# The last two tiles of a fused projection kernel: broad passes of both first, then the narrow ones, and the last store issued by another engine

## The chip, the cores and the metric

The kernel runs on one core of a Trainium2 chip. A core has five engines that run their own instruction streams and meet through semaphores: TensorE (PE in the profile; its weight loads are listed apart as PEld), VectorE (DVE), ScalarE (ACT), GpSimd (POOL) and SyncE (SP), which here only issues transfers. The metric is the device time of one execution in microseconds, as a median over several runs.

## The reference, cut to what matters

The input x has 128 rows of the batch, 32 steps and 512 features, all in float32. For each element there is a base projection, a low-rank correction (LoRA) of two experts out of eight, chosen per token from logits with a bias for the row's own expert, a second projection by a matrix of signs, and the residual.

```python
base = jnp.einsum('btd,od->bto', x, W)
logits = jnp.einsum('btd,ed->bte', x, Wr) + bias[:, None, :]
topw, topi = jax.lax.top_k(logits, TOP_K)
weights = jax.nn.softmax(topw, axis=-1)
gates = jnp.sum(jax.nn.one_hot(topi, E) * weights[..., None], axis=-2)
h = jnp.einsum('btd,erd->bter', x, A)
lora_out = jnp.einsum('bter,bte,eor->bto', h, gates, B)
y = base + SCALING * lora_out
x = x + jnp.einsum('bsi,io->bso', y, sign) * jax.nn.softplus(scale)
```

## The kernel before, in words

**Tiles.** A tile is one step t of x: 128 batch rows by 512 features. There are 32 tiles (`TILES`), numbered 0 to 31. In its first 21 us the kernel multiplies W by the signs into one 512 by 512 matrix that also holds the residual, and B by the signs into b2. What is left for a tile is one product with a matrix `wide` of 648 columns, 8 for the logits, 128 for h (8 experts of rank 16) and 512 for the output, and one LoRA sum, the gated h times b2, added on top.

**Passes.** Each float32 product is made as three products of high and low parts (hi·hi, hi·lo, lo·hi), for each of four chunks of 128 features: 12 passes. The result of a tile lies in two PSUM banks: bank 0 holds logits, h and the first 256 output columns (8 + 128 + 256 = 392 columns), bank 1 the other 256 (`BANKS`). In the usual step each of the 12 passes is issued for bank 0 (392 columns) and then for bank 1 (256 columns), with a weight load before each. Three tiles have banks at a time: `pair[n]`, n = tile mod 3; tile 28 and tile 31 share pair 1.

**What a tile goes through.** SyncE loads x, VectorE transposes it in blocks (L428), ScalarE makes the high part (L352), GpSimd the low part (L303), TensorE makes the passes (`wide`, L630). When bank 0 is complete (`head_ready`), VectorE adds the bias to the logits (L510), takes the maxima (L518, L523), works out the two weights together with ScalarE's exponential (L384) and gates h (`h_gated`, L542). TensorE transposes h (`turn_h`, L654) into the single bank p_ht, ScalarE takes the high part (`ht_hi`, L380), VectorE the low part (`ht_lo`, L501), and TensorE adds the LoRA sum (`lora`, L647, six 256-column passes in both banks). ScalarE copies the output to SBUF in two halves (L393, L394) and SyncE stores it (L230).

**The order.** It is written out by hand for each engine, in `step`. In step s TensorE makes the first half of tile s's passes, the LoRA sum of tile s-2, the second half, and the transposition of tile s-1's h. ScalarE in step s: ht_hi of tile s-2, exponential of tile s-1, the output copy of tile s-2. VectorE in step s: logits and gating of tile s-1, and ht_lo of tile s-2; from step 31 on ("hurry") ht_lo stands behind the search for the maxima, and ahead of the rest of the gating, before that ahead of the maxima.

**The end.** TensorE runs steps 0 to 30 and then `finish` (L679) for tile 31. There bank 0 is made in two parts: first the 136 columns of logits and h alone, so that the gating can begin, then, interleaved with the LoRA sums and transpositions of the tiles before, the 256 columns of bank 1 and last the 256 output columns of bank 0. The last LoRA sum is done for bank 0 first, which VectorE copies (L552) and SyncE stores (L237), and then for bank 1, which ScalarE copies (L394) and SyncE stores (L239). SyncE then waits for all stores (L274 to L276).

Of the kernel before, what the change touches and what calls it, by code (L numbers as in the profile page):

```python
# [18 lines left out]
def adaln_ffn_kernel(nc: bass.Bass, x, lang_ids, W, Wr, A, B, sign, scale, out):  # L19
# [13 lines left out]
    BATCH, TILES, D = x.shape  # L33
# [4 lines left out]
    KC = D // P  # L38
    OC = O // P
    HEAD = E + ER  # L40
    WIDE = HEAD + D
    Y0 = D // 2
    BANKS = ((0, 0, HEAD + Y0), (1, HEAD + Y0, WIDE))
    assert BATCH == P and ER == P and D % (NQ * Q) == 0 and HEAD + Y0 <= 512 and O == KC * P
    WARM_UPS = 18
    S3 = 3
# [10 lines left out]
    with ctx:  # L57
        def sb(name, shape, dt=FP32):
            return ctx.enter_context(nc.sbuf_tensor(name, shape, dt))

        def sem(name):
            return ctx.enter_context(nc.semaphore(name))
# [47 lines left out]
        second = sb("second", [P, E])  # L110
# [4 lines left out]
        y = [sb(f"y{n}", [P, D]) for n in range(S3)]  # L115
# [48 lines left out]
        y_stored = [sem(f"y_stored{n}") for n in range(S3)]  # L164
        xt_made = sem("xt_made")
        xt_hi_made = sem("xt_hi_made")
        xt_lo_made = sem("xt_lo_made")
        head_ready = sem("head_ready")
# [13 lines left out]
        ht_lo_made = sem("ht_lo_made")  # L182
        y_summed = sem("y_summed")
        y_copied = sem("y_copied")
# [9 lines left out]
        def slot(r, d=0):  # L194
            return (r + d) % S3
# [5 lines left out]
        LAG = 2  # L201
# [4 lines left out]
        def steps(eng, step, end=TILES + LAG):  # L206

            for s in range(FIRST):
                step(s // S3, s % S3, s)
            with eng.Fori(1, 1 + LOOPS) as q:  # L210
                for r in range(FIRST - S3, FIRST):
                    step(q, r, None)
            for s in range(AFTER, end):
                step(s // S3, s % S3, s)
# [5 lines left out]
        @block.sync  # L220
        def _(sp_eng):
            def load(q, r, t):
                for i in range(NQ):
                    sp_eng.dma_start(x_in[r % S3][Q * i:Q * i + Q, :, :], x_load[i, :, t, :, :])\
                        .then_inc(x_loaded[r % S3], 16)

            def store(q, r, d):

                sp_eng.wait_ge(y_copied, S3 * q + r + d + 1)
                sp_eng.dma_start(out[:, S3 * q + r + d, :], y[slot(r, d)][:, :])\  # L230
                    .then_inc(y_stored[slot(r, d)], 16)

            def store_last():

                n = (TILES - 1) % S3
                sp_eng.wait_ge(last_copied, 1)
                sp_eng.dma_start(out[:, TILES - 1, 0:Y0], y[n][:, 0:Y0]).then_inc(last_stored, 16)  # L237
                sp_eng.wait_ge(y_copied, TILES)
                sp_eng.dma_start(out[:, TILES - 1, Y0:D], y[n][:, Y0:D]).then_inc(y_stored[n], 16)  # L239

            for j in range(OC):
                sp_eng.dma_start(w_in[:, j, :], w_load[:, j, :]).then_inc(w_loaded[j], 16)  # L242
                if j == 1:
                    sp_eng.dma_start(scale_in[:, :], scale.partition_broadcast(P)).then_inc(scale_loaded, 16)
            load(0, 0, 0)
            for i in range(NQ):
                sp_eng.dma_start(a_in[Q * i:Q * i + Q, :, :], a_load[i, :, :, :]).then_inc(a_loaded, 16)

            sp_eng.wait_ge(wr_zeroed, 1)
            for i in range(NQ):  # L250
                sp_eng.dma_start(wr_in[Q * i:Q * i + E, :], wr_load[i, :, :]).then_inc(wr_loaded, 16)
            sp_eng.dma_start(b_in[:, :, :], b_load).then_inc(b_loaded, 16)
            sp_eng.dma_start(ids_in[:, :], lang_ids.rearrange("(p a) -> p a", a=1)).then_inc(ids_loaded, 16)
            for t in range(1, S3):
                load(0, t, t)

            def turnover(q, r, s):

                if s is None or s + S3 < TILES:
                    sp_eng.wait_ge(xt_made, S3 * q + r + 1)  # L260
                    load(q, r, S3 * q + r + S3)
                if s is None or s >= LAG + LEAD:
                    store(q, r, -LAG - LEAD)

            for s in range(LAG + LEAD):
                turnover(s // S3, s % S3, s)
            loops = (TILES - S3 - LAG - LEAD) // S3
            with sp_eng.Fori(1, 1 + loops) as q:
                for r in range(LAG + LEAD - S3, LAG + LEAD):
                    turnover(q, r, None)  # L270
            for s in range(LAG + LEAD + S3 * loops, TILES + LAG + LEAD - 1):
                turnover(s // S3, s % S3, s)
            store_last()
            sp_eng.wait_ge(last_stored, 16)  # L274
            for n in range(S3):
                sp_eng.wait_ge(y_stored[n], 16 * len(range(n, TILES, S3)))  # L276
# [49 lines left out]
        def _(act):  # L326
# [69 lines left out]
                    high_x(q, r, LEAD, first=(s is not None and s + LEAD < S3))  # L396

            steps(act, step)

        @block.vector  # L400
        def _(dve):
# [155 lines left out]
        def _(pe):  # L557
# [63 lines left out]
            def wide(r, chunks, cols, opens=False, signals=False):  # L621

                n = slot(r)
                for k in chunks:
                    for l, w in ((xt_hi[n], wide_hi), (xt_hi[n], wide_lo), (xt_lo[n], wide_hi)):
                        for bank, lo, hi in cols:
                            at0 = lo - BANKS[bank][1]
                            last = nc.tensor.matmul(pair[n][bank][:, at0:at0 + hi - lo], l[:, k, :], w[:, k, lo:hi],  # L630
                                                    start=(opens and k == 0 and l is xt_hi[n] and w is wide_hi),
                                                    stop=False, skip_group_check=True)
                            if signals and k == KC - 1 and l is xt_lo[n]:

                                last.then_inc((head_ready, wide_done)[bank], 1)
                return last
# [5 lines left out]
            def lora(n, banks):  # L642

                for l, w, stop in ((ht_hi, b2_hi, False), (ht_hi, b2_lo, False), (ht_lo, b2_hi, True)):
                    for bank in banks:
                        o = pair[n][bank][:, (HEAD, 0)[bank]:(HEAD + Y0, D - Y0)[bank]]
                        last = nc.tensor.matmul(o, l[:, :], w[:, (0, Y0)[bank]:(Y0, D)[bank]],  # L647
                                                start=False, stop=stop, skip_group_check=True)
                return last

            def turn_h(done):

                pe.wait_ge(h_gated_made, done)
                nc.tensor.transpose(p_ht[:, 0:P], h_gated[:, :], ident[:, :]).then_inc(ht_turned, 1)  # L654
# [23 lines left out]

            def finish(s):  # L679

                r, n = s % S3, s % S3
                everything = range(KC)
                pe.wait_ge(xt_lo_made, s + 1)
                pe.wait_ge(y_copied, s - S3 + 1)
                wide(r, everything, ((0, 0, HEAD),), opens=True).then_inc(head_ready, 1)
                pe.wait_ge(ht_lo_made, s - LAG + 1)
                lora(slot(r, -LAG), (0, 1)).then_inc(y_summed, 1)
                wide(r, range(KC // 2), (BANKS[1],), opens=True)
                turn_h(s)  # L690
                wide(r, range(KC // 2, KC), (BANKS[1],))
                pe.wait_ge(ht_lo_made, s)
                lora(slot(r, -1), (0, 1)).then_inc(y_summed, 1)
                turn_h(s + 1)
                wide(r, everything, ((0, HEAD, HEAD + Y0),))
                pe.wait_ge(ht_lo_made, s + 1)
                lora(n, (0,)).then_inc(last_summed, 1)
                lora(n, (1,)).then_inc(y_summed, 1)
# [1 line left out]

            pe.wait_ge(head_lo_made, 1)
            pe.wait_ge(ident_made, 1)
            steps(pe, step, TILES - 1)
            finish(TILES - 1)

# [22 lines left out]
```

## Time and profile before

| | us |
|---|---|
| median of 3 runs | 170.25 (170.19 to 170.54) |
| the profiled execution | 169.39 |
| its span in the profile | 167.6 |

| engine | busy us | share of the span |
|---|---|---|
| TensorE, matmuls | 159.8 | 95% |
| TensorE, weight loads | 154.5 | 92% |
| VectorE | 99.0 | 59% |
| ScalarE | 65.8 | 39% |
| GpSimd | 51.6 | 31% |

Of the chain of work that ended last, TensorE has 79% of the span, VectorE 11%, transfers 5% (at the start) and ScalarE 2%.

How to read it: the start of a matmul in the trace and the start of the next one tell the pace. The length of one matmul record is longer than the pace, since matmuls are pipelined. All times of the trace count from the start of the span; what lies outside of the span (169.39 against 167.6) is seen in no row. "x2" in a row of the timeline means that two neighbouring instructions are merged.

### The profile page before, as it was taken

The numbers are of one execution on the slowest core, as the hardware profiler recorded it, in microseconds if no ns is written. First come the engines' busy times: TensorE is split into PE (matmuls) and PEld (weight loads), VectorE is DVE, ScalarE is ACT, GpSimd is POOL, SyncE is SP. The second block draws the span as 40 slices with busy tenths as digits, with TensorE's granted clock in tenths as the row PEclk, the third lists the DMA queues.
The fourth block names the chain that finished last, engine by engine and source line by source line (L and its number), as shares of the span: only waits on it lengthen the run. The fifth ranks groups of instructions, "written<-read, shape, count | busy, mean of one in ns | idle before, by whom it ended". The sixth has DMA issues, their size and how long they took to land.

```text
span 167.6 us, 3738 instructions
## 1 busy us (share of the span) xinstructions
PE 159.8 (95%) x1082; PEld 154.5 (92%) x1082; DVE 99.0 (59%) x421; ACT 65.8 (39%) x177; POOL 51.6 (31%) x48
## 2 busy tenths in 40 slices
PE   7698998799999999999999999999999999999993
PEld 5476897799999999999999999999999999999982
DVE  5379999665555555555555555555555555555451
ACT  3363453233444444443444344443333334444240
POOL 2676275033333333333322222223333333333000
PEclk9999999999999999999999999999999999999999
DMA  4799113133433333333333333333333333111113
GB/s 140 227 296 186 32 27 111 56 129 124 129 127 125 125 125 125 125 119 109 111 108 115 116 122 124 111 124 123 112 125 123 112 125 125 63 63 66 65 63 125
DMA packets 26311, 19.51 MB, mean 116 GB/s; under 512 B 4128, under 2 KB 21312, under 8 KB 26304
## 3 DMA queue, kind: packets, MB, share of 16 engines
q1 hardware_dynamic: 25728, 18.38, 36.0%
q10 hardware_dynamic: 576, 1.05, 1.7%
q8 instruction: 3, 0.05, 0.1%
q14 instruction: 4, 0.03, 0.1%
HBM read 11.03 MB, written 8.39 MB: 116 GB/s over the span
## 4 chain that ended last, share of the span: by engine, by line
PE 79%; DVE 11%; DMA 5%; ACT 2%; issue 1%; SPq 1%; DVEq 0%
PE pair L630 64%; PE pair L647 13%; DMA w_in<-in_L_cond_W 5%; PE p_ht L654 2%; DVE xt L428 2%; DVE second L533 1%; DVE w_lo L418 1%; DVE m_full L477 1%; ACT wide_hi L367 1%; DVE bias L492 1%; DVE sp L446 1%; DVE sp L449 1%; DVE top_no L528 1%; SPq L242 0%; DVE b_lo L495 0%
## 5 line engine op out<-in xcount | busy, mean ns | idle before, releaser
L303 POOL TENSOR_TENSOR xt_lo<-xt,xt_hi 128x512 fp32r<-128x512 f32 x32 | 41.4, 1294 | 92.2 <-ACT xt_hi L352 92.1
L630 PE MATMUL pair<-wide_hi,xt_hi 128*128 128x256 f32 (+2 forms) x260 | 62.8, 318 | 0.0
L630 PE MATMUL pair<-wide_hi,xt_lo 128*128 128x256 f32 (+2 forms) x260 | 60.4, 310 | 0.0
L630 PE MATMUL pair<-wide_lo,xt_hi 128*128 128x256 f32 (+2 forms) x260 | 60.3, 309 | 0.0
L630 PEld LDWEIGHTS pair<-wide_hi,xt_lo 128*128 128x128 f32 x260 | 40.3, 188 | 0.0
L630 PEld LDWEIGHTS pair<-wide_hi,xt_hi 128*128 128x128 f32 x260 | 40.2, 189 | 0.1
L630 PEld LDWEIGHTS pair<-wide_lo,xt_hi 128*128 128x128 f32 x260 | 40.2, 188 | 0.0
L393 ACT ACTIVATE y<-pair 128x256 f32<-128x256 f32 x31 | 11.9, 384 | 44.6 <-PE pair L647 44.6
L510 DVE TENSOR_TENSOR logits<-pair,bias 128x8 f32<-128x8 f32 x32 | 5.3, 164 | 35.6 <-PE pair L630 35.6
L428 DVE STREAM_TRANSPOSE xt<-x_in 128x512 f32<-128x512 f32 x32 | 22.7, 711 | 3.7 <-DVE top L518 3.2
L352 ACT ACTIVATE xt_hi<-xt 128x512 fp32r<-128x512 f32 x32 | 20.3, 634 | 5.4 <-DVE xt L428 5.4
L380 ACT ACTIVATE ht_hi<-p_ht 128x128 fp32r<-128x128 f32 x32 | 8.9, 277 | 23.4 <-PE p_ht L654 23.4
L501 DVE TENSOR_TENSOR ht_lo<-p_ht,ht_hi 128x128 fp32r<-128x128 f32 x32 | 9.3, 291 | 14.6 <-ACT ht_hi L380 14.6
L384 ACT ACTIVATE e<-top 128x1 f32<-128x1 f32 x32 | 9.5, 295 | 14.4 <-DVE top L518 14.4
L542 DVE SCALAR_TENSOR_TENSOR h_gated<-pair,rdenom,gate 128x128 f32<-128x128 f32 x32 | 11.2, 350 | 3.3
L647 PE MATMUL pair<-b_hi,ht_hi 128*128 128x256 f32 x64 | 13.1, 283 | 0.0
L647 PE MATMUL pair<-b_lo,ht_hi 128*128 128x256 f32 x64 | 12.9, 280 | 0.0
L394 ACT ACTIVATE y<-pair 128x256 f32<-128x256 f32 x32 | 12.2, 380 | 1.8 <-PE pair L647 1.8
L647 PE MATMUL pair<-b_hi,ht_lo 128*128 128x256 f32 x64 | 12.8, 279 | 0.0
L654 PE MATMUL p_ht<-ident,h_gated 128*128 128x128 f32 x32 | 8.8, 275 | 1.7 <-DVE h_gated L542 1.6
L533 DVE TENSOR_SCALAR second<-expert_no,top_no,e 128x8 f32<-128x8 f32 x32 | 10.2, 320 | 0.0
L647 PEld LDWEIGHTS pair<-b_hi,ht_hi 128*128 128x128 f32 x64 | 9.8, 188 | 0.2 <-DVE ht_lo L501 0.2
(79 smaller groups left out, 136.7 us busy)
## 6 DMA issues: line engine op xcount, KB each, us to landing
x_in<-in_x SPq DMA_DIRECT2D x128, 64.0 KB, 1.9
out<-y SPq DMA_DIRECT2D x31, 256.0 KB, 2.1
sign_in<-in_L_ffn_sign ACTq DMA_DIRECT2D x4, 256.0 KB, 6.9
w_in<-in_L_cond_W SPq DMA_DIRECT2D x4, 256.0 KB, 7.0
a_in<-in_L_cond_A SPq DMA_DIRECT2D x4, 64.0 KB, 5.8
b_in<-in_L_cond_B SPq DMA_DIRECT2D x1, 256.0 KB, 5.3
out<-y SPq DMA_DIRECT2D x2, 128.0 KB, 1.8
wr_in<-in_L_cond_Wr SPq DMA_DIRECT2D x4, 4.0 KB
```

Of the source, the lines that this page charges most:

```text
L303: nc.gpsimd.tensor_tensor(xt_lo[n][:, :, :].rearrange("p j (g b) -> p g j b", g=NQ), xt[n][:, :, :, :], xt_hi[n][:, :, :].bitcast(FP32).re ...
L352: nc.scalar.activation(xt_hi[n][:, :, :].rearrange("p j (g b) -> p g j b", g=NQ), xt[n][:, :, :, :], ACT.Copy).then_inc(xt_hi_made, 1)
L384: nc.scalar.activation(e2[:, :], top[:, 0:1], ACT.Exp, bias=top[:, 1:2], scale=-1.0)\
L393: nc.scalar.activation(y[n][:, 0:Y0], pair[n][0][:, HEAD:HEAD + Y0], ACT.Copy)
L394: nc.scalar.activation(y[n][:, Y0:D], pair[n][1][:, 0:D - Y0], ACT.Copy).then_inc(y_copied, 1)
L428: nc.vector.transpose(xt[n][:, :, :, :].rearrange("p g j b -> p (g j b)"), x_in[n][:, :, :].rearrange("p g c -> p (g c)")).then_inc(xt_mad ...
L501: nc.vector.tensor_tensor(ht_lo[:, :], p_ht[:, 0:P], ht_hi[:, :].bitcast(FP32), ALU.subtract)\
L533: nc.vector.tensor_scalar(second[:, :], expert_no[:, :], top_no[:, 1:2], e2[:, 0:1], ALU.is_equal, ALU.mult).then_inc(second_made, 1)
L542: nc.vector.scalar_tensor_tensor(h_gated[:, :].rearrange("p (e r) -> p e r", e=E), pair[n][0][:, E:HEAD].rearrange("p (e r) -> p e r", e=E ...
L630: last = nc.tensor.matmul(pair[n][bank][:, at0:at0 + hi - lo], l[:, k, :], w[:, k, lo:hi], start=(opens and k == 0 and l is xt_hi[n] and w ...
L647: last = nc.tensor.matmul(o, l[:, :], w[:, (0, Y0)[bank]:(Y0, D)[bank]], start=False, stop=stop, skip_group_check=True)
L654: nc.tensor.transpose(p_ht[:, 0:P], h_gated[:, :], ident[:, :]).then_inc(ht_turned, 1)
```

## The change

TensorE's usual steps end one tile earlier, and `finish` now holds tiles 30 and 31. The 392-column passes (bank 0) of tile 30 come first, then those of tile 31, each in two halves with the LoRA sum of tile 28 or 29 between them, and a transposition behind each; then the 256-column passes (bank 1) of tile 30, its LoRA sum, the first chunk (three passes) of tile 31's bank 1, the transposition of tile 31's h, the other nine passes, and the last LoRA sum. The split of the last tile's bank 0 into 136 and 256 columns is gone. On SyncE the store of the second half of the last tile is taken out; ScalarE issues it behind its last copy, after a wait for that copy.

```diff
             def store_last():
 
                 n = (TILES - 1) % S3
                 sp_eng.wait_ge(last_copied, 1)
                 sp_eng.dma_start(out[:, TILES - 1, 0:Y0], y[n][:, 0:Y0]).then_inc(last_stored, 16)
-                sp_eng.wait_ge(y_copied, TILES)
-                sp_eng.dma_start(out[:, TILES - 1, Y0:D], y[n][:, Y0:D]).then_inc(y_stored[n], 16)
...
             steps(act, step)
+            act.wait_ge(y_copied, TILES)
+            act.dma_start(out[:, TILES - 1, Y0:D], y[(TILES - 1) % S3][:, Y0:D])\
+                .then_inc(y_stored[(TILES - 1) % S3], 16)
...
             def finish(s):
 
-
-                r, n = s % S3, s % S3
-                everything = range(KC)
+                before, r, n = (s - 1) % S3, s % S3, s % S3
+                first, second = range(KC // 2), range(KC // 2, KC)
+
+                pe.wait_ge(xt_lo_made, s)
+                pe.wait_ge(y_copied, s - S3)
+                wide(before, first, (BANKS[0],), opens=True)
+                pe.wait_ge(ht_lo_made, s - LAG)
+                lora(slot(before, -LAG), (0, 1)).then_inc(y_summed, 1)
+                wide(before, second, (BANKS[0],)).then_inc(head_ready, 1)
+                turn_h(s - 1)
+
                 pe.wait_ge(xt_lo_made, s + 1)
                 pe.wait_ge(y_copied, s - S3 + 1)
-                wide(r, everything, ((0, 0, HEAD),), opens=True).then_inc(head_ready, 1)
+                wide(r, first, (BANKS[0],), opens=True)
                 pe.wait_ge(ht_lo_made, s - LAG + 1)
                 lora(slot(r, -LAG), (0, 1)).then_inc(y_summed, 1)
-                wide(r, range(KC // 2), (BANKS[1],), opens=True)
+                wide(r, second, (BANKS[0],)).then_inc(head_ready, 1)
                 turn_h(s)
-                wide(r, range(KC // 2, KC), (BANKS[1],))
+
+                wide(before, range(KC), (BANKS[1],), opens=True)
                 pe.wait_ge(ht_lo_made, s)
-                lora(slot(r, -1), (0, 1)).then_inc(y_summed, 1)
+                lora(before, (0, 1)).then_inc(y_summed, 1)
+                wide(r, range(1), (BANKS[1],), opens=True)
                 turn_h(s + 1)
-                wide(r, everything, ((0, HEAD, HEAD + Y0),))
+                wide(r, range(1, KC), (BANKS[1],))
                 pe.wait_ge(ht_lo_made, s + 1)
                 lora(n, (0,)).then_inc(last_summed, 1)
                 lora(n, (1,)).then_inc(y_summed, 1)
...
-            steps(pe, step, TILES - 1)
+            steps(pe, step, TILES - 2)
             finish(TILES - 1)
```

The rows below are TensorE's instructions. `pair10` is bank 0 of pair 1 (tiles 28 and 31), `pair01` bank 1 of pair 0 (tile 30), and so on. First the place behind the second half of tile 30's passes, before the change:

```order
L630 MATMUL pair00<-wide_hi,xt_lo0 128x392
L630 MATMUL pair01<-wide_hi,xt_lo0 128x256
L654 MATMUL p_ht<-ident,h_gated 128x128 [waits h_gated_made]
L630 MATMUL pair10<-wide_hi,xt_hi1 128x136 [waits y_copied,xt_lo_made]
L630 MATMUL pair10<-wide_lo,xt_hi1 128x136
```

The same place after it:

```order
L631 MATMUL pair00<-wide_hi,xt_lo0 128x392
L655 MATMUL p_ht<-ident,h_gated 128x128 [waits h_gated_made]
L631 MATMUL pair10<-wide_hi,xt_hi1 128x392 [waits y_copied,xt_lo_made]
L631 MATMUL pair10<-wide_lo,xt_hi1 128x392
```

Tile 30's passes no longer carry their 256-column halves, and tile 31 begins with 392 columns in place of 136; the lines of the changed file count one further.

Then the place around the transposition of tile 30's h, before the change, where it stands inside tile 31's bank-1 passes:

```order
L630 MATMUL pair11<-wide_hi,xt_lo1 128x256
L654 MATMUL p_ht<-ident,h_gated 128x128 [waits h_gated_made]
L630 MATMUL pair11<-wide_hi,xt_hi1 128x256
L630 MATMUL pair11<-wide_lo,xt_hi1 128x256
L630 MATMUL pair11<-wide_hi,xt_lo1 128x256
```

After it, behind tile 31's 392-column passes:

```order
L631 MATMUL pair10<-wide_hi,xt_lo1 128x392
L655 MATMUL p_ht<-ident,h_gated 128x128 [waits h_gated_made]
L631 MATMUL pair01<-wide_hi,xt_hi0 128x256
L631 MATMUL pair01<-wide_lo,xt_hi0 128x256
L631 MATMUL pair01<-wide_hi,xt_lo0 128x256
```

Before, six passes stood between this transposition and the LoRA sum of tile 30 that needs its result; now twelve, those of tile 30's bank 1.

## Rows read from the trace of the kernel before

**Rows 1.** The page: TensorE's granted clock in 40 slices, in tenths.
```profile
PEclk9999999999999999999999999999999999999999
```
**Rows 2.** The chain in order of time: start us, us, what.
```profile
161.85 0.36 DVE h_gated L542
```
**Rows 3.** The timeline, TensorE, tile 30: start us, us, engine, line, operation.
```profile
152.93 0.27 PE L654 MATMUL p_ht<-ident,h_gated 128*128 128x128 f32 x1
...
155.53 0.45 PE L630 MATMUL pair<-wide_hi,xt_hi 128*128 128x392 f32 x2
...
157.01 0.46 PE L630 MATMUL pair<-wide_hi,xt_lo 128*128 128x392 f32 x2
157.31 0.27 PE L654 MATMUL p_ht<-ident,h_gated 128*128 128x128 f32 x1
```
**Rows 4.** The timeline, TensorE, tile 31.
```profile
157.48 0.28 PE L630 MATMUL pair<-wide_lo,xt_hi 128*128 128x136 f32 x1
...
158.60 0.28 PE L630 MATMUL pair<-wide_hi,xt_lo 128*128 128x136 f32 x1
...
159.23 0.41 PE L647 MATMUL pair<-b_hi,ht_lo 128*128 128x256 f32 x2
159.47 0.28 PE L630 MATMUL pair<-wide_hi,xt_hi 128*128 128x256 f32 x1
...
160.06 0.28 PE L630 MATMUL pair<-wide_hi,xt_lo 128*128 128x256 f32 x1
```
**Rows 5.** The timeline, TensorE, 512-column passes while the matrices are made.
```profile
18.20 0.39 PE L561 MATMUL pair<-sign_lo,w_hi 128*128 128x512 f32 x1
18.43 0.39 PE L562 MATMUL pair<-sign_hi,w_lo 128*128 128x512 f32 x1
```
**Rows 6.** The timeline, TensorE's late weight loads, the last LoRA sum; in brackets idle before.
```profile
161.14 0.30 PEld L647 LDWEIGHTS pair<-b_hi,ht_hi 128*128 128x128 f32 x2 [0.19 <-DVE ht_lo L501]
...
162.26 0.14 PEld L654 LDWEIGHTS p_ht<-ident,h_gated 128*128 128x128 f32 x1 [0.35 <-DVE h_gated L542]
...
163.84 0.28 PE L647 MATMUL pair<-b_hi,ht_hi 128*128 128x256 f32 x1
```
**Rows 7.** The timeline, VectorE and ScalarE on tiles 28 to 31.
```profile
153.62 0.29 DVE L501 TENSOR_TENSOR ht_lo<-p_ht,ht_hi 128x128 fp32r<-128x128 f32 x1 [0.44 <-ACT ht_hi L380]
...
155.15 0.35 DVE L542 SCALAR_TENSOR_TENSOR h_gated<-pair,rdenom,gate 128x128 f32<-128x128 f32 x1
...
156.01 0.38 ACT L394 ACTIVATE y<-pair 128x256 f32<-128x256 f32 x1
...
157.39 0.17 DVE L510 TENSOR_TENSOR logits<-pair,bias 128x8 f32<-128x8 f32 x1 [1.89 <-PE pair L630]
...
157.95 0.27 DVE L501 TENSOR_TENSOR ht_lo<-p_ht,ht_hi 128x128 fp32r<-128x128 f32 x1
...
158.99 0.35 DVE L542 SCALAR_TENSOR_TENSOR h_gated<-pair,rdenom,gate 128x128 f32<-128x128 f32 x1
...
162.70 0.28 ACT L380 ACTIVATE ht_hi<-p_ht 128x128 fp32r<-128x128 f32 x1
...
163.01 0.29 DVE L501 TENSOR_TENSOR ht_lo<-p_ht,ht_hi 128x128 fp32r<-128x128 f32 x1 [0.81 <-ACT ht_hi L380]
```
**Rows 8.** The timeline, the last copy and the last stores.
```profile
164.75 0.38 ACT L394 ACTIVATE y<-pair 128x256 f32<-128x256 f32 x1 [1.77 <-PE pair L647]
164.85 0.33 SPq L237 DMA_DIRECT2D out<-y  x1
165.22 0.43 SPq L239 DMA_DIRECT2D out<-y  x1
```
**Rows 9.** By line: ScalarE's issues (durations ns), their landing, and the last store's landing.
```profile
L329 ACTq DMA_DIRECT2D sign_in<-in_L_ffn_sign x4: 407/454/557, 0.7 to 2.1; - x4
...
DMA to landing us min/median/max: 4.2/6.9/8.6
...
DMA to landing us min/median/max: 1.8/1.8/1.8
```

## Prediction

> **What bounds the kernel now.** I read the page first. TensorE runs at full granted clock in every slice [rows 1], and the chain that ended last goes through its matmuls from the first tile to the last, with a short detour through VectorE and ScalarE near the end. So what counts is the time that TensorE needs from tile to tile and the places where it waits. In the chain by time the last detour shows: the gating of the last tile, ended by h_gated [rows 2]. All tiles up to 29 are untouched by the change, so I take as anchor the transposition of tile 28's h that closes them, at 152.93 [rows 3], and follow TensorE to the first matmul of the last LoRA sum, at 163.84 [rows 6]: 10.91 us. Behind that point the work is the same in both kernels up to the last store.
>
> **Prices of TensorE's work, from the distances between starts.** Tile 30 in its old form alternates a 392-column and a 256-column pass: five such pairs from 155.53 to 157.01 [rows 3], 0.296 a pair. The 136-column passes of tile 31: ten from 157.48 to 158.60 [rows 4], 0.112 each. Lone 256-column passes: five from 159.47 to 160.06 [rows 4], 0.118. A LoRA sum is six 256-column passes, a pair from 159.23 to 159.47, so 0.71. From the transposition at 152.93 to the second half of tile 30 at 155.53 [rows 3] go 2.60; six pairs (1.78) and a LoRA sum (0.71) leave 0.11 for a transposition. No row has 392-column passes in a row. Subtraction gives 0.296 - 0.118 = 0.178. A line through the 256-column row (0.118) and the 512-column rows (18.20 to 18.43, 0.227 [rows 5]) gives 0.176. I take 0.178; the far end is 0.227, the row of the 512-column pass, since fewer columns should not cost more.
>
> The 136-column pass is the odd one: by the line through 256 and 512 columns it should be 0.067, and it is 0.112. So something other than its columns sets it, and I read it as its weight load. The Trainium skill, "TensorE: Matmul & The Clock Gate", section "Back-to-back issue gap", gives N/2.4 + 2.5 ns for a lone pass, 59 ns at 136 columns; its section "LDWEIGHTS" gives P/1.2, 107 ns for 128 columns. By the first rule the change would save 12 x (59 - (166 - 109)) = 24 ns of TensorE's work; the row agrees with the second, and decides.
>
> **Before, on the path:** four transpositions 0.44, twelve pairs 3.55, twelve 136-column passes 1.34, twenty-four 256-column passes 2.83, three LoRA sums 2.13: 10.29. Of 10.91 that leaves 0.62 of waiting: idle times of 0.19 and 0.35 of the weight loads ahead of the LoRA sum of tile 30 and the last transposition [rows 6], and the restarts.
>
> **After, the work:** tiles 30 and 31 both take twelve 392-column passes, 24 x 0.178 = 4.27, and the same 24 256-column ones; the 136-column passes and the twelve 256-column ones of the last tile's first bank are gone. 0.44 + 4.27 + 2.83 + 2.13 = 9.67. The work is 0.62 shorter.
>
> **After, the waits.** This is where the order could fail, so I lay it on the clock, each matmul group after the other from 152.93. First half of tile 30: 153.04 to 154.11. LoRA sum of 28: to 154.82. Second half: to 155.89, transposition of tile 29's h: to 156.00. First half of 31: to 157.07. LoRA sum of 29: to 157.78. Second half: to 158.85, transposition of 30: to 158.96. 256-column passes of 30: to 160.38. LoRA sum of 30: to 161.09. Three passes of 31: to 161.44. Transposition of 31: to 161.55. Nine passes: to 162.61. Each group wants its weights some 0.11 earlier than its matmul, and a finished result reaches TensorE 0.05 later (h_gated ends at 162.21 [rows 2], the load starts at 162.26 [rows 6]).
> LoRA sum of 28 wants ht_lo at 154.00. It ends at 153.91 [rows 7], usable 153.96: slack 0.04, where it had 0.7 before.
> Tile 29's h_gated ends at 155.50 [rows 7], wanted 155.78: no wait.
> Tile 31 needs the bank of tile 28 copied out. ScalarE's second copy began 0.48 after the matmul that follows the LoRA sum (156.01 [rows 7] against 155.53 [rows 3]); now 155.30, ending 155.68, usable 155.73, wanted 155.89. Slack 0.16.
> LoRA sum of 29: the logits began 0.38 after the start of the last 392-column pass (157.39 [rows 7] against 157.01). Now that pass starts at 155.71, the logits at 156.09. VectorE ended ht_lo 0.83 after the logits' start (157.95 + 0.27 [rows 7]): 156.92, usable 156.97, wanted 156.96. It just binds, 0.01.
> Tile 30's h_gated ended 1.95 after the logits' start (158.99 + 0.35 [rows 7]): 158.04, wanted 158.74. No wait. LoRA sum of 30: logits of tile 31 at 159.05, ht_lo 159.88, wanted 160.27. No wait; this is the first stall of before, gone because the transposition now stands ahead of twelve passes, not six.
> Tile 31's h_gated: 159.05 + 1.95 = 161.00, usable 161.05, wanted 161.33. No wait. Before, it was late since ht_lo of tile 30 stands ahead of the gating on VectorE and waited for a transposition at 160.18; now that runs at 158.85.
> Last LoRA sum: ScalarE must first copy tile 30's output, second copy from 161.57 to 161.95, and takes ht_hi of tile 31 behind it or a little under its end. From ht_hi's start to ht_lo's end went 0.60 (162.70 to 163.30 [rows 7]). Usable between 162.49 and 162.60, wanted 162.50. So 0 to 0.1 late; with the 0.01 above I book 0.04 in all. The last LoRA sum starts at 162.65, against 163.84: **1.19 us earlier**, 0.62 from work and 0.57 from waits.
>
> **The store.** ScalarE's copy of the last half starts 0.91 behind the last LoRA sum and ends at 165.13; SyncE issues the store at 165.22, right behind its store of the first half, which holds it to 164.85 + 0.33 = 165.18 [rows 8]. ScalarE's own queue is free, so the issue may come at 0.04 or 0.05 behind the copy: at most 0.05 won. ScalarE's four issues at the start took 0.407 to 0.557, median 0.454; SyncE's here took 0.43 [rows 8, 9]. Landing came 1.8 after the issue [rows 9]; I keep that. Bounds: 0.1 better, if the issue is as short as SyncE's lone 0.33, and 0.13 worse by the longest of ScalarE's; the nearest row is the 0.454, so I take the 0.05 gained less 0.02. Nothing is queued behind this issue on ScalarE but its end. SyncE's final waits are the same.
> The Trainium skill, "DMA: Bandwidth & Descriptors", section "Issuing engines are not separate DMA queues", says that a second issuing engine saves only the sequencer's time. No row here shows two stores of the two engines side by side.
>
> **Sum.** 1.19 + 0.03 = 1.22. The profiled execution took 169.39 with a span of 167.6; it should become 168.17 and 166.4. The median of the runs shown, 170.25, is 0.86 above the profiled one; the same step puts it at 169.03.
>
> **Rivals.**
> Thin waits bind. Five waits have 0.04 to 0.3 of slack where they had more, and the last is under nothing. If each of the three tightest (LoRA sums of 28, 29, 31) comes 0.1 late, and the copy of tile 28 as well, 0.4 is lost: 169.4. For it: the slack is of the size of my reading errors, and one late transposition moves all behind it. Against: they take offsets that are equal in rows of different tiles.
> ScalarE's store is somewhat dearer than SyncE's: 0.13 to 0.3 worse, 169.2 to 169.3.
> The store from ScalarE ends the kernel late (slower than before). Its queue has carried nothing since the first microseconds, and there the shortest landing was 4.2 [rows 9]. At 163.99 + 4.2 = 168.2 against 167.0 it would cost 1.2 net: 171.4. It decides from a landing over 3.0. Against: those four shared the engines with SyncE's loads; a free store landed in 1.8.
> The 392-column passes cost up to 0.227 when alone: 24 x 0.049 = 1.18 dearer, and the gain is gone: 170.2. Against: two ways to size them agree within 0.002.
> A pass goes by its columns, so the 136-column ones were cheap: at 0.067 each the work saved is 12 x (0.067 - 0.060) = 0.08 instead of 0.62, and the time 169.6. The rows of twelve passes at 0.112 speak against it. This is also what the page's gap rule would have.
> All goes a bit better: 0.1 less for the issue, 0.176 a pass, no late LoRA sum: 168.8.
>
> **How the numbers follow.** Forecast, within 0.15 of 169.03: 0.62. Thin waits: 0.17. Dearer store: 0.08. Better: 0.07. Passes up to 0.227 (most of it near no change): 0.02. By columns: 0.01. Late store: 0.03. The range 168.7 to 169.6 takes in all but the last ones and the scatter of the runs (170.19 to 170.54 before). A measurement of this kernel can tell about 0.2%, 0.34 us, from no change; all but the passes at 0.227 and the late store are faster by more: faster 0.94, same 0.03, slower 0.03.
>
> **What would show it.** In the changed profile: 392-column passes 0.178 apart; no idle of a weight load above 0.1 behind the anchor; the last LoRA sum 9.7 behind the anchor instead of 10.9; the gating of tile 31 ending before TensorE asks for it; ScalarE's issue within 0.1 of its copy's end, landing 1.8 later. Wrong would be: a new wait ahead of the LoRA sum of 28 or 29 of more than 0.1, a pace above 0.185, or a landing above 2.1.

## The result and the profile after

| | before | changed |
|---|---|---|
| median of 6 runs | 170.22 us | 168.91 us (168.49 to 169.22) |
| ratio to before | | 0.9918, 95% interval 0.9903 to 0.9933 |
| profiled execution, its span | 169.39, 167.6 | 169.07, 167.2 |

The medians differ by 1.31 us; the interval of the ratio stands for 1.14 to 1.65. The profiled executions alone differ by 0.32 only, and that has to be explained before anything else is read. The chain in order of time, near the start of each kernel (columns: start us, us, what), first before:

```profile
2.12 7.70 DMA w_in<-in_L_cond_W
```

and the changed kernel:

```profile
2.12 8.64 DMA w_in<-in_L_cond_W
```

The same load of W took 0.94 longer in the profiled execution of the changed kernel, and the anchor, the transposition that closes the last usual step, came 0.96 later: at 153.89, where it was at 152.93 [rows 3]. The change touches nothing ahead of it. In the eleven traces of this study the anchor lay between 152.93 and 154.12. In ten of them the chain waited 7.70 to 8.84 for this load, and the anchor less the wait is 145.2 to 145.3 in each; in the eleventh, that of the moved transposition below, the chain starts with a load of x instead, and the anchor is at 153.67. The profiled execution of before had the shortest wait of all, which fits its 169.39 under a median of 170.2. So from here on all intervals are counted from the anchor, and the start does not enter them.

The end of the changed kernel, the chain in order of time:

```profile
154.05 0.11 PE p_ht L655
154.16 1.07 PE pair L631 x6
155.23 0.71 PE pair L648 x6
155.94 1.09 PE pair L631 x6
157.03 0.11 PE p_ht L655
157.14 1.07 PE pair L631 x6
158.22 0.71 PE pair L648 x6
158.93 1.06 PE pair L631 x6
159.99 0.11 PE p_ht L655
160.10 1.43 PE pair L631 x12
161.53 0.71 PE pair L648 x6
162.24 0.36 PE pair L631 x3
162.59 0.11 PE p_ht L655
162.71 1.06 PE pair L631 x9
163.77 0.72 PE pair L648 x6
164.49 0.02 issue
164.51 0.38 ACT y L392
```

Where the chain of before left TensorE for VectorE [rows 2], this one stays on it to the last LoRA sum, and there is no "issue" between its pieces: TensorE does not wait. None of its weight loads behind the anchor has idle time before it. (The chain dates a piece by the ends of its matmuls, so its times are about 0.16 later than the starts in the timeline.)

The timeline has the starts that answer to [rows 3 to 6]:

```profile
153.89 0.27 PE L655 MATMUL p_ht<-ident,h_gated 128*128 128x128 f32 x1
...
154.18 0.34 PE L631 MATMUL pair<-wide_lo,xt_hi 128*128 128x392 f32 x1
...
154.89 0.34 PE L631 MATMUL pair<-wide_hi,xt_lo 128*128 128x392 f32 x1
...
162.44 0.27 PE L655 MATMUL p_ht<-ident,h_gated 128*128 128x128 f32 x1
...
163.61 0.28 PE L648 MATMUL pair<-b_hi,ht_hi 128*128 128x256 f32 x1
```

Lone 392-column passes are 0.178 apart (four from 154.18 to 154.89). From the anchor to the last LoRA sum go 163.61 - 153.89 = **9.72**, before 10.91. From there to the end of the span 3.59 (before 3.76). In all 13.31 against 14.67, 1.36 less.

The last copy and the two stores, which answer to [rows 8]:

```profile
164.51 0.38 ACT L392 ACTIVATE y<-pair 128x256 f32<-128x256 f32 x1 [1.41 <-PE pair L648]
164.62 0.33 SPq L237 DMA_DIRECT2D out<-y  x1
164.93 0.36 ACTq L398 DMA_DIRECT2D out<-y  x1
```

ScalarE issues 0.04 behind its copy and takes 0.36 for it; SyncE's second issue came 0.09 behind the copy and took 0.43. The landing is 1.8 behind the issue in both.

### The profile page after: what moved, and what is told of

It reads as the page before. It is cut to its first block, busy times and chain, and to the rows that moved or that the text cites. A ratio compares the mean times of both kernels' runs of the same rounds, so it can differ in the third digit from the quotient of the medians.

```text
span 167.2 us, 3714 instructions
## 1 busy us (share of the span) xinstructions
PE 159.2 (95%) x1070; PEld 153.5 (92%) x1070; DVE 100.0 (60%) x421; ACT 66.1 (40%) x177; POOL 51.3 (31%) x48
## 4 chain that ended last, share of the span: by engine, by line
PE 80%; DVE 10%; DMA 5%; ACT 1%; issue 1%; SPq 1%; DVEq 0%
PE pair L631 64%; PE pair L648 14%; DMA w_in<-in_L_cond_W 5%; PE p_ht L655 2%; DVE xt L429 2%; DVE w_lo L419 1%; DVE m_full L478 1%; ACT wide_hi L365 1%; DVE bias L493 1%; DVE sp L447 1%; DVE second L534 1%; DVE sp L450 1%; DVE top_no L529 1%; SPq L240 0%; DVE b_lo L496 0%
## 5 line engine op out<-in xcount | busy, mean ns | idle before, releaser
L631 PE MATMUL pair<-wide_hi,xt_hi 128*128 128x392 f32 (+1 forms) x256 | 62.7, 320 | 0.0
L631 PE MATMUL pair<-wide_hi,xt_lo 128*128 128x392 f32 (+1 forms) x256 | 60.1, 311 | 0.0
L631 PE MATMUL pair<-wide_lo,xt_hi 128*128 128x392 f32 (+1 forms) x256 | 60.1, 311 | 0.0
L631 PEld LDWEIGHTS pair<-wide_hi,xt_lo 128*128 128x128 f32 x256 | 39.8, 188 | 0.0
L631 PEld LDWEIGHTS pair<-wide_hi,xt_hi 128*128 128x128 f32 x256 | 39.6, 189 | 0.2
L631 PEld LDWEIGHTS pair<-wide_lo,xt_hi 128*128 128x128 f32 x256 | 39.7, 188 | 0.0
```

## The experiments

In what follows an interval is the one from the anchor to the first matmul of the last LoRA sum, and the tail what is left of the span behind it. (Where that matmul itself had waited, it is dated 0.355, three passes, ahead of the fourth one.) The shares of the change first, then the thin waits, then the price of a narrow pass.

### The order alone and the store alone

The changed kernel with the store back on SyncE:

```diff
             steps(act, step)
-            act.wait_ge(y_copied, TILES)
-            act.dma_start(out[:, TILES - 1, Y0:D], y[(TILES - 1) % S3][:, Y0:D])\
-                .then_inc(y_stored[(TILES - 1) % S3], 16)
```

> The new order on TensorE, with the last store left on SyncE. Measured in the trace from the anchor (the transposition of tile 28's h that closes the last usual step) to the first matmul of the last LoRA sum: 10.91 us before, 9.72 in the changed kernel; and from there to the end of the span: 3.76 before, 3.59 in the changed kernel. My theory: the order carries 1.19 us and the store little. Expected here: 9.72 to the last LoRA sum, and 3.76 behind it if the 0.17 by which the changed kernel's tail is shorter comes from the store (3.59 if it has another cause). SyncE's second issue should take 0.43 again, being right behind the first. Time some 1.0 to 1.2 us below before. Rival (the store matters most): 10.9 and 3.59.

Measured: interval 163.01 - 153.34 = 9.67, tail 3.8, ratio to before 0.9928 (0.9908 to 0.9948), median 168.94 against 170.16. So the order carries what the runs can see. TensorE does the same here as in the changed kernel, whose interval is 9.72: two traces of one order can differ by 0.05, and smaller differences between intervals say nothing. SyncE's issues there:

```profile
164.02 0.33 SPq L237 DMA_DIRECT2D out<-y  x1
164.40 0.43 SPq L239 DMA_DIRECT2D out<-y  x1
```

The kernel of before with only the store moved:

```diff
-                sp_eng.wait_ge(y_copied, TILES)
-                sp_eng.dma_start(out[:, TILES - 1, Y0:D], y[n][:, Y0:D]).then_inc(y_stored[n], 16)
...
             steps(act, step)
+            act.wait_ge(y_copied, TILES)
+            act.dma_start(out[:, TILES - 1, Y0:D], y[(TILES - 1) % S3][:, Y0:D])\
+                .then_inc(y_stored[(TILES - 1) % S3], 16)
```

> The order of before, with only the last store moved to ScalarE. Expected: 10.91 from the anchor to the last LoRA sum, and 3.59 to 3.62 behind it, ScalarE's issue 0.36 long and 0.04 behind its copy. Time 0.15 below before, which is at the edge of what the runs can tell. If the shorter tail of the changed kernel has another cause: 3.76.

Measured: interval 164.97 - 154.05 = 10.92, tail 3.6, ratio 0.9999 (0.9987 to 1.0010). The issue is again short:

```profile
166.29 0.36 ACTq L398 DMA_DIRECT2D out<-y  x1
```

Over all traces the tail is 3.70 to 3.79 in the five kernels that store from SyncE and 3.59 to 3.66 in the six that store from ScalarE, some 0.12 less. The spans are given to 0.1 only, but the starts are finer: from the first matmul of the last LoRA sum to the last issue go 1.38 or 1.39 in the five and 1.31 or 1.32 in the six, and that issue takes 0.43 or 0.36. So about half comes from the earlier issue and half from the shorter one. In the times of whole runs that cannot be told from nothing.

### The work alone, in the old order

```diff
-                wide(r, everything, ((0, 0, HEAD),), opens=True).then_inc(head_ready, 1)
+                wide(r, everything, (BANKS[0],), opens=True).then_inc(head_ready, 1)
...
                 turn_h(s + 1)
-                wide(r, everything, ((0, HEAD, HEAD + Y0),))
                 pe.wait_ge(ht_lo_made, s + 1)
```

> The order of before, but tile 31's bank 0 is made whole, in twelve 392-column passes, at the place of the 136-column ones, and the 256-column ones at the end are gone: the saving of work alone. If only TensorE's work counted: 10.91 - 0.62 = 10.29. My theory: nothing then stands behind the last transposition, so its chain to ht_lo is bare. Laid on the clock of before: logits of tile 31 at 159.76; LoRA sum of 30 waits 0.26 for ht_lo; h_gated ends at 163.02, the last transposition waits 0.4; the last LoRA sum starts at 164.25. So 11.3 from the anchor, 0.4 slower than before (0.25 to 0.55).

Measured: interval 164.48 - 153.15 = 11.33 and a ratio of 1.0020 (1.0006 to 1.0033), slower than before by 0.1 to 0.6 us though TensorE has 0.6 less to do. Its weight loads show where that went:

```profile
162.16 0.30 PEld L647 LDWEIGHTS pair<-b_hi,ht_hi 128*128 128x128 f32 x2 [0.19 <-DVE ht_lo L501]
...
163.28 0.14 PEld L654 LDWEIGHTS p_ht<-ident,h_gated 128*128 128x128 f32 x1 [0.35 <-DVE h_gated L542]
...
164.38 0.19 PEld L647 LDWEIGHTS pair<-b_hi,ht_hi 128*128 128x128 f32 x1 [0.96 <-DVE ht_lo L501]
```

The two waits of before are all there, and a third of 0.96, the bare chain from the last transposition to ht_lo. In the old order the saving of work is lost again: the 256-column passes of the last tile's bank 0 stood behind that transposition and covered its chain. The changed kernel puts most of tile 31's bank 1 there.

### The work given back, in the new order

```diff
-                wide(r, first, (BANKS[0],), opens=True)
+                for k in first:
+                    wide(r, [k], ((0, 0, HEAD),), opens=True)
+                    wide(r, [k], ((0, HEAD, HEAD + Y0),))
...
-                wide(r, second, (BANKS[0],)).then_inc(head_ready, 1)
+                for k in second:
+                    wide(r, [k], ((0, HEAD, HEAD + Y0),))
+                    last = wide(r, [k], ((0, 0, HEAD),))
+                last.then_inc(head_ready, 1)
```

> The changed kernel, but each 392-column pass of tile 31 is made as one of 136 and one of 256 columns at the same place, so that the order of waits stays and the work of before comes back. Theory (a pass of 136 columns costs 0.112, what its weight load costs): 12 x (0.112 + 0.118 - 0.178) = 0.62 more, 10.34 from the anchor to the last LoRA sum, with no waits. Rival (a pass goes by its columns, so the 0.62 of the sum was never in the work): 0.08 more, 9.80. Time by the theory 0.6 below before.

Measured: interval 164.39 - 154.12 = 10.27, 0.55 more than the changed kernel (0.60 more than the run of the order alone); ratio 0.9968 (0.9958 to 0.9978), 0.54 below before. The rival by which a pass goes by its columns had 0.08. So in the new order the gain parts into 0.55 to 0.60 for the work and 10.91 - 10.27 = 0.64 for the waits.

### One transposition moved, in the old order

The prediction laid the waits of before on the place of tile 30's transposition. This run moves it alone:

```diff
-                wide(r, range(KC // 2), (BANKS[1],), opens=True)
                 turn_h(s)
-                wide(r, range(KC // 2, KC), (BANKS[1],))
+                wide(r, everything, (BANKS[1],), opens=True)
```

> The order and the passes of before (136 and 256 columns), with one move: the transposition of tile 30's h stands ahead of the twelve bank-1 passes of tile 31, not between their halves. Theory: the two waits of before, 0.62 in all, come from the place of this one transposition: it holds up ht_lo of tile 30, and behind it on VectorE and ScalarE the gating of tile 31. On the clock of before: transposition at 159.47, ht_hi at 159.78, the exponential of tile 31 from 159.96, h_gated ends near 161.2; the LoRA sum of 30 ends at 161.7. No wait is left: 10.91 - 0.62 = 10.29 from the anchor to the last LoRA sum, 0.6 below before. Rival (the second wait is the bare chain from tile 31's logits, whatever the place of the transposition): only the first wait goes, 0.25, so 10.66.

Measured: interval 164.33 - 153.67 = 10.66, not 10.29; ratio 0.9989 (0.9977 to 1.0001). The interval is 0.37 longer than my theory said. The number is the rival's, but the timeline shows another reason than the rival's bare chain:

```profile
160.22 0.28 PE L654 MATMUL p_ht<-ident,h_gated 128*128 128x128 f32 x1
...
160.42 0.38 ACT L393 ACTIVATE y<-pair 128x256 f32<-128x256 f32 x1 [1.58 <-PE pair L647]
...
160.70 0.38 ACT L394 ACTIVATE y<-pair 128x256 f32<-128x256 f32 x1
...
160.96 0.28 ACT L380 ACTIVATE ht_hi<-p_ht 128x128 fp32r<-128x128 f32 x1
...
161.12 0.30 ACT L384 ACTIVATE e<-top 128x1 f32<-128x1 f32 x1
...
162.34 0.35 DVE L542 SCALAR_TENSOR_TENSOR h_gated<-pair,rdenom,gate 128x128 f32<-128x128 f32 x1
...
162.74 0.14 PEld L654 LDWEIGHTS p_ht<-ident,h_gated 128*128 128x128 f32 x1 [0.31 <-DVE h_gated L542]
```

The transposition came early, but ScalarE was busy with the two copies of tile 29's output, whose LoRA sum had just ended, and took ht_hi 0.43 later than it could. The exponential and VectorE's ht_lo are behind it, and the gating of tile 31 behind both. The chain in order of time goes through the second copy:

```profile
160.70 0.38 ACT y L394
161.08 0.18 ACT ht_hi L380
```

It is not so in the kernel before. There the copies ended at 160.33, ht_hi began 0.30 behind its late transposition, as soon as it can, and the chain goes from the transposition straight to it:

```profile
160.34 0.12 PE p_ht L654
...
160.48 0.29 ACT ht_hi L380
...
160.79 0.29 DVE ht_lo L501
```

So the copies were no cause of the waits of before; the move ran into them. Counted from the anchor, the transposition came 0.70 earlier than before (6.55, not 7.25), ht_hi only 0.26 earlier (7.29, not 7.55) and h_gated of tile 31 0.25 earlier (8.67, not 8.92). The last transposition starts some 0.05 behind the end of h_gated in both kernels and TensorE waits for nothing after it, so the interval gained the same 0.25.

The next run has one difference from this one, the place of those copies on ScalarE:

```diff
+                if s == TILES:
+                    n = (TILES - 3) % S3
+                    act.wait_ge(y_summed, TILES - 2)
+                    act.wait_ge(y_stored[n], 16 * ((TILES - 3) // S3))
+                    nc.scalar.activation(y[n][:, 0:Y0], pair[n][0][:, HEAD:HEAD + Y0], ACT.Copy)
+                    nc.scalar.activation(y[n][:, Y0:D], pair[n][1][:, 0:D - Y0], ACT.Copy).then_inc(y_copied, 1)
-                if has(s, -LAG):
+                if has(s, -LAG) and s != TILES - 1:
```

> The moved transposition of before gave 10.66 from the anchor, one wait less and not two. In that trace ScalarE's two copies of tile 29's output (160.42 to 161.08) stand between the transposition (160.22) and its ht_hi (160.96, in place of 160.53), and hold up ht_lo of tile 30, the exponential and the gating of tile 31 by 0.43. Here ScalarE makes those copies behind ht_hi of tile 30 and the exponential of tile 31; all else is as in that kernel. Theory (the place in ScalarE's queue makes the second wait): h_gated of tile 31 is seen 0.05 ahead of when TensorE wants it, and the interval is 10.28. Rival (the bare chain from the logits to the gating sets the second wait): 10.66 again.

Measured: interval 163.70 - 153.40 = 10.30, ratio 0.9973 (0.9961 to 0.9985). ht_hi now comes 0.31 behind its transposition, at 160.25 against 159.94:

```profile
160.25 0.28 ACT L380 ACTIVATE ht_hi<-p_ht 128x128 fp32r<-128x128 f32 x1 [1.69 <-PE p_ht L660]
...
160.42 0.28 ACT L384 ACTIVATE e<-top 128x1 f32<-128x1 f32 x1
...
160.61 0.37 ACT L390 ACTIVATE y<-pair 128x256 f32<-128x256 f32 x1
...
161.62 0.35 DVE L548 SCALAR_TENSOR_TENSOR h_gated<-pair,rdenom,gate 128x128 f32<-128x128 f32 x1
```

So the wait that was left in the run before this one was ScalarE's order, not the length of the chain from the logits. With the transposition moved and the copies out of its way, 0.61 of the 0.62 of waiting is gone in the old order: the place of that transposition was the cause of both waits. (What this kernel still has over the changed one, 10.30 against 9.72, is the work of the split: a second measurement of it, 0.58.) In the changed kernel six 392-column passes stand between the LoRA sum of 29 and tile 30's transposition, and ScalarE's copies fall into them: they start at 158.96 and 159.24 and are done at 159.62, the transposition is at 159.83.

### Two thin waits, moved past their limit

The LoRA sum of tile 28 one chunk earlier:

```diff
-                wide(before, first, (BANKS[0],), opens=True)
+                wide(before, range(1), (BANKS[0],), opens=True)
...
-                wide(before, second, (BANKS[0],)).then_inc(head_ready, 1)
+                wide(before, range(1, KC), (BANKS[0],)).then_inc(head_ready, 1)
```

> The changed kernel with the LoRA sum of tile 28 behind the first chunk (three passes) of tile 30, not the second. By my clock its weights are wanted at 0.53 behind the anchor and ht_lo is usable at 1.03 (154.87 + 0.05 against the anchor 153.89), so TensorE waits 0.50 and nothing gives it back: 10.22 from the anchor to the last LoRA sum, against 9.72. Rival (the weight load or the queue hides part of a wait): 9.9 to 10.1.

Measured: interval 164.04 - 153.84 = 10.20, the wait in full and nothing given back.

```profile
154.88 0.51 PE L648 MATMUL pair<-b_hi,ht_hi 128*128 128x256 f32 x2 [0.23 <-DVE ht_lo L502]
```

The idle time in the brackets is about half of the 0.48 that is lost, since the matmul record before still runs when the wait has begun; the row of the weight load ahead of it has 0.55. The loss is read from the distances between starts.

The last transposition one chunk later:

```diff
-                wide(r, range(1), (BANKS[1],), opens=True)
+                wide(r, range(2), (BANKS[1],), opens=True)
                 turn_h(s + 1)
-                wide(r, range(1, KC), (BANKS[1],))
+                wide(r, range(2, KC), (BANKS[1],))
```

> The changed kernel with the last transposition behind two chunks (six passes) of tile 31's bank 1, not one. Its chain (0.31 to ht_hi, 0.61 to the end of ht_lo, 0.05 to be seen) then ends 0.27 behind the time at which the last LoRA sum wants its weights: 9.99 from the anchor. If the chain were shorter than I read it: 9.72.

Measured: interval 163.54 - 153.61 = 9.93, 0.21 more than the changed kernel and 0.06 less than expected; 0.04 of that lies ahead of the transposition, which came 8.87 behind the anchor, where 8.91 were reckoned.

```profile
163.44 0.19 PEld L648 LDWEIGHTS pair<-b_hi,ht_hi 128*128 128x128 f32 x1 [0.19 <-DVE ht_lo L502]
```

Three passes are 0.35, but only 0.28 of the move reaches ht_lo: in the changed kernel ScalarE's copy of tile 30 held ht_hi to 0.38 behind the transposition, here it came 0.30 behind. The changed kernel itself has next to no slack at this place; its ht_lo ends at 163.43 and the weight load starts at 163.49, on time:

```profile
162.82 0.28 ACT L378 ACTIVATE ht_hi<-p_ht 128x128 fp32r<-128x128 f32 x1
...
163.14 0.29 DVE L502 TENSOR_TENSOR ht_lo<-p_ht,ht_hi 128x128 fp32r<-128x128 f32 x1 [1.17 <-ACT ht_hi L378]
...
163.49 0.19 PEld L648 LDWEIGHTS pair<-b_hi,ht_hi 128*128 128x128 f32 x1
```

Each of the two kernels was run once (169.51 and 168.99), and they are read from their traces alone.

### The price of a narrow pass

```diff
-                wide(before, range(KC), (BANKS[1],), opens=True)
+                wide(before, range(KC), ((1, HEAD + Y0, HEAD + Y0 + 64),), opens=True)
```

> The changed kernel, but the twelve bank-1 passes of tile 30 have 64 columns in place of 256, so that 192 output columns of tile 30 lack their product. Theory (a narrow pass costs what its weight load costs): starts 0.112 apart, as with 136 columns, 9.65 from the anchor. Rival (it goes by columns): starts 0.04 apart, and TensorE then waits for ht_lo of tile 30; some 9.0 to 9.4.

Measured, in one run (168.43): interval 162.97 - 153.34 = 9.63, where the rival that goes by columns had 9.0 to 9.4.

```profile
159.42 0.28 PE L631 MATMUL pair<-wide_lo,xt_hi 128*128 128x64 f32 x1
...
160.54 0.28 PE L631 MATMUL pair<-wide_hi,xt_lo 128*128 128x64 f32 x1
```

Ten passes from 159.42 to 160.54 are 0.112 each, as with 136 columns [rows 4]. A pass with its own weight load costs 0.112 whether it has 64 or 136 columns, 0.118 with 256, 0.178 with 392 and 0.227 with 512.
## Why the prediction was right, point by point

**The sum.** Forecast 169.03, measured 168.91. Its clock said 9.72 from the anchor to the last LoRA sum, and the trace has 9.72. To the last digit that is luck, since the same order took 9.67 in the run of the order alone. From the anchor to the end the traces gained 1.36, where the sum had 1.22; the difference is nearly all the store.

**The prices.** 0.178 for a lone 392-column pass, got by subtraction, is what the trace has. The work was worth 0.62 in the sum; the runs have 0.55 to 0.60. The gap is small and has a place: 136- and 256-column passes in turn took 1.39 and 1.33 for twelve each in the run that gives the work back, 2.72 together, where 12 x (0.112 + 0.118) is 2.76.

**The waits.** That both waits of before would go was right, 0.62 reckoned and 0.61 to 0.64 found. That LoRA sums 28, 29 and the last one would just hold was right: none of them shows idle time. Whether the 0.04 booked for lateness was needed can't be told from traces that differ by 0.05. The rival of thin waits was right that the slack is thin (moving either of two waits by one chunk costs 0.48 and 0.21), but it was enough.

**The condition that was left out.** The prediction named the cause of the second wait as VectorE's ht_lo of tile 30 standing ahead of the gating and waiting for a late transposition. The trace of before and the two runs in the old order bear that out. What it didn't say is that an earlier transposition helps only if ScalarE is free to take ht_hi: with the LoRA sum of tile 29 right ahead of it, the copies of tile 29 come in between, and of 0.62 only 0.25 is won. I had looked at ScalarE's copies only for tiles 28 and 30. It did not hurt the forecast, since the new order puts six passes between that LoRA sum and the transposition, but I had not checked that, and in that respect the forecast was lucky.

**The store.** Sized at 0.03, found at 0.12 over all traces, inside the bounds (at most 0.05 for the earlier issue and up to 0.1 for a shorter one). The mis-sized term is the issue: I took 0.454, the median of ScalarE's four issues at the start, and it was 0.36, near SyncE's lone 0.33. The rows of the start were back-to-back issues of other transfers, and SyncE's 0.43 was right behind another issue too; the lone stores at the end are shorter on either engine. The late store (4.2) did not come: it landed in 1.8 from a queue that had been idle since the start.

**The median.** I moved the profiled execution and the median by the same step. That held, but the profiled pair alone would have shown 0.32. What saved the comparison was the anchor.

## What to carry to other kernels

When a chain of small steps runs beside a bound engine, put each step's launch where its helpers' queues are empty, and check every engine that the chain crosses, not only the one that is named as the releaser. Splitting a product into a narrow and a broad part costs more than its columns (0.112 for 136 columns here, where a line through the broader passes gives 0.067), so whole passes of the next tile are the cheaper filler. To compare two traces of kernels that share their start, count from the last event that the change does not touch.

## What the runs showed of the hardware that I had not expected

Columns were all but free at the narrow end: 64 and 136 columns both cost 0.112 a pass, 256 columns 0.118. SyncE's issue of a store of y takes 0.33 to 0.38 with nothing right ahead of it and 0.43 right behind another issue (139.13 and 165.22 in the trace of before); ScalarE's lone one takes 0.36. And the first load of W varies by 1.1 us from trace to trace (in ten of them the chain waited 7.70 to 8.84 for it), which is nearly the whole effect of this change. That it also makes most of the scatter of the times is likely but not shown, since each kernel has one trace.
